# Windowed attention and a gated recurrence on one core: the softmax division moved into the layout of the values product

## What is computed

```python
qkv = einsum('bse,fe->bsf', x, w_in)                   # q, k, v
scores = einsum('bhnqd,bhnkd->bhnqk', q, k2) / sqrt(D) + slope[h] * delta, -inf outside the window
o = einsum('bhnqk,bhnkd->bhnqd', softmax(scores), v2)  # k2, v2: own block and the one before
x1 = layernorm(x + o @ w_out.T)
def step(c, xt):                                        # 16 steps of 512 rows
    ft = sigmoid(xt @ wf.T + c @ uf.T + bf); it = sigmoid(...); gt = tanh(...)
    return ft * c + it * gt
h = tanh(x1 @ wo.T + c_final @ uo.T + bo)
out = layernorm(x1 + h)
```

## Time and profile before

| | before |
|---|---|
| median of 3 runs | 994.17 us (993.75 to 994.33) |
| the profiled execution, its own time | 994.83 us |
| its span | 992.7 us |
| mean granted clock of TensorE | 0.955 |
| TensorE busy | 911.2 us, 92% |
| VectorE busy | 714.1 us, 72% |
| ScalarE busy | 574.8 us, 58% |
| GpSimd busy | 409.0 us, 41% |
| bytes moved | 131.86 MB, mean 133 GB/s |

### The profile page before, as it was taken

How to read it: one execution, slowest core, us unless ns; L and a number is a source line. 1 busy time by engine, 2 the same in 40 slices (tenths; PEclk the granted TensorE clock), 3 DMA queues, 4 the chain that set the end, 5 groups by cost and what they waited for, 6 DMA issues and landing times. The chain is left out here.

```text
span 992.7 us, 25986 instructions
## 1 busy us (share of the span) xinstructions
PE 911.2 (92%) x9500; PEld 749.7 (76%) x9500; DVE 714.1 (72%) x2795; ACT 574.8 (58%) x1167; POOL 409.0 (41%) x687
## 2 busy tenths in 40 slices
PE   3587889999999999999999999999999999989994
PEld 2365668888888888888888888888787876668884
DVE  7666677878787868787878787878787754337875
ACT  6044556565656565656565656565656554335786
POOL 6143343444535353535353535354444443001443
PEclk8586989999999999999999999999999989899998
DMA  7644454535454545353645454645444400131764
GB/s 265 164 124 127 131 139 132 151 122 156 124 151 128 145 134 150 123 154 125 153 128 151 128 143 137 149 131 147 133 121 138 119 23 22 44 106 46 215 204 131
DMA packets 93534, 131.86 MB, mean 133 GB/s; under 512 B 12128, under 2 KB 47584, under 8 KB 93408
## 3 DMA queue, kind: packets, MB, share of 16 engines
q1 hardware_dynamic: 93136, 129.95, 45.3%
q10 hardware_dynamic: 272, 0.26, 0.1%
HBM read 79.31 MB, written 50.33 MB: 131 GB/s over the span
## 5 line engine op out<-in xcount | busy, mean ns | idle before, releaser
L689 DVE CUSTOM_DVE_ANT_0 bank<-bank,mask 128x256 f32<-128x256 f32 (+1 forms) x1024 | 369.4, 423 | 130.7 <-PE bank L951 128.7
L448 ACT ACTIVATE Pt<-bank 128x512 f32<-128x512 f32 (+1 forms) x512 | 248.2, 536 | 193.4 <-PE bank L972 193.3
L347 POOL TENSOR_SCALAR_AFFINE_SELECT Pt<-Pt 128x512 f32<-128x512 f32 x256 | 170.4, 666 | 403.9 <-ACT Pt L448 403.9
L951 PE MATMUL bank<-Ks,Qs 59*128 59x256 f32 (+1 forms) x1024 | 148.2, 319 | 44.9 <-DVE max_q L689 31.3
L951 PEld LDWEIGHTS bank<-Ks,Qs 59*128 59x128 f32 x1024 | 107.3, 191 | 86.6 <-DVE max_q L689 42.5
L689 DVE DVE_READ_ACCUMULATOR2_ANT max_q<- 128x1 f32 x1024 | 144.9, 142 | 0.0
L349 POOL TENSOR_SCALAR_AFFINE_SELECT Pt<-Pt 128x384 f32<-128x384 f32 x256 | 144.7, 565 | 0.0
L986 PE MATMUL bank<-Pt,Vp 128*32 128x256 f32 (+1 forms) x2048 | 130.9, 377 | 0.0
L932 PE MATMUL bank<-x1T,Wg 64*128 64x512 f32 x960 | 127.9, 398 | 1.0 <-DVE o_tok L703 1.0
L932 PE MATMUL bank<-cT,Ug 64*128 64x512 f32 x960 | 125.7, 393 | 0.0
L972 PE MATMUL bank<-Qs,Ks 60*128 60x256 f32 (+1 forms) x1024 | 111.8, 271 | 0.7 <-ACT Pt L448 0.3
(11 more groups left out here) (111 smaller groups left out, 1354.7 us busy)
## 6 DMA issues: line engine op xcount, KB each, us to landing
parts_dram<-qk_parts SPq DMA_DIRECT2D x128, 256.0 KB
Qs<-parts_dram SPq DMA_DIRECT2D x128, 128.0 KB, 2.7
Ks<-parts_dram SPq DMA_DIRECT2D x128, 128.0 KB, 2.8
xt_raw<-in_xt SPq DMA_DIRECT2D x16, 512.0 KB, 4.5
Qs<-parts_dram SPq DMA_DIRECT2D x128, 64.0 KB, 2.7
Ks<-parts_dram SPq DMA_DIRECT2D x128, 64.0 KB, 2.7
x_res<-in_x SPq DMA_DIRECT2D x16, 512.0 KB, 3.9
x_dram<-y SPq DMA_DIRECT2D x16, 512.0 KB, 4.4
```

Source lines behind the costliest of these rows:

```text
L347: gp.affine_select(out=p4[:, :, 0:128], in_=p4[:, :, 0:128], compare_op=ALU.is_ge, fill=0.0, base=0, pattern=[[0, 4], [1, 128]], channel_m ...
L448: sc.activation(probabilities(g, 2 * pair + odd)[:, S * a:S * a + n], SC[odd][:, 0:n], ACT.Exp).then_inc(exp_done, 1)
L689: ins = ve.tensor_tensor_reduce(out=raw, in0=raw, in1=mask[:, keys], scale=1.0, scalar=MASKED, op0=ALU.add, op1=ALU.max, accum_out=max_q[: ...
L951: ins = te.matmul(MX[odd][:, 256 * (n % 2):256 * (n % 2) + 256][:, keys], Qs[rows, 2 * g + pair, n * WIN:(n + 1) * WIN], Ks[rows, 2 * g + ...
```

## The change

1. **Division in the layout of the values product.** `ctx_out` is followed by a store of ctx_raw to DRAM, issued by ScalarE, which waits for its own copy. SP fetches the context rows of two quads at a time into o_un (`load_contexts`) and the denominators, 16 rows for each quarter of a sequence, into den_q (`load_denominators`). VectorE transposes den_q in blocks of 32 x 32, takes reciprocals, transposes back. SP stores the inverses and reads them back, each row spread over the 16 rows of its head (`store_inverses`, `spread_inverses`). GpSimd multiplies (`scale_contexts`), and the product is already in the layout of oT. The context and output transposes of TensorE and `normalise` remain for the last sequence alone.
2. **SP's order.** The inverses go in front of `parts_to_dram(t + 1, 1)`; the second stack goes in front of the next input's load.
3. **Swap.** The second query/key pair is projected in slots 9 and 10, the values projection in slots 11 and 12; the low parts `qk_lo` of the pair stand between the maxima of slots 10, 11 and 12 (before: 12, 13 and 14). The transposes of x1 precede values and maxima in slot 13. Banks are handed on in another rotation.
4. **Input parts.** From sequence 2 on the high parts of x are made two sequences ahead in slots 13 and 14, and the low parts by GpSimd, in front of the last two windows of quad 1.
5. **Buffers and weights.** To make room, Wo and Uo share Win's memory and are loaded and split at the end of the loop, on ScalarE and GpSimd.

```diff
@@ sync
+            def load_denominators(t):
+                sp.wait_ge(den_cleared, 1)
+                for g in range(QUADS):
+                    wait(sp, ctx_stored[g], 16, t, 16)
+                wait(sp, inv_stored, 16, t - 1, 16)
+                rows = ctx_dram[t % 2].rearrange("g (h r) (q i) -> q (g h) r i", r=2 * D, i=128)[:, :, D, :]
+                for q in range(4):
+                    sp.dma_start(den_q[32 * q:32 * q + H, :], rows[q]).then_inc(den_in, 16)
+            def load_contexts(t, c):
+                for g in (2 * c, 2 * c + 1):
+                    wait(sp, ctx_stored[g], 16, t, 16)
+                wait(sp, otlo_done, 2, t - 1, c + 1)
+                rows = ctx_dram[t % 2, 2 * c:2 * c + 2].rearrange("g (h r) s -> (g h) r s", r=2 * D)[:, 0:D, :]
+                sp.dma_start(o_un[:, c, :], rows).then_inc(o_un_in[c], 16)
+            def store_inverses(t):
+                wait(sp, inv_turned, 1, t, 1)
+                sp.dma_start(inv_dram[t % 2].rearrange("r (q i) -> q r i", i=128), den_q[:, :]).then_inc(inv_stored, 16)
+            def spread_inverses(t):
+                wait(sp, inv_stored, 16, t, 16)
+                for c in range(KC):
+                    wait(sp, scaled_done, 2, t - 1, c + 1)
+                    rows = inv_dram[t % 2, 8 * c:8 * c + 8]
+                    sp.dma_start(inv_den[:, c, :], rows.unsqueeze(1).to_broadcast([8, D, S])).then_inc(inv_in[c], 16)
...
+                if now: stack(t, 2)
+                if by_rows: load_contexts(t - 1, 0)
                 if real(t + 2): load_xt(t + 2)
...
+                if by_rows: load_denominators(t - 1)
                 if n1: stack(t + 1, 0)
+                if by_rows: load_contexts(t - 1, 1)
                 if now: max_to_stack(t, 2)
+                if by_rows:
+                    store_inverses(t - 1)
+                    spread_inverses(t - 1)
                 if n1: parts_to_dram(t + 1, 1)
@@ gpsimd
+            def scale_contexts(t, c):
+                wait(pool, o_un_in[c], 16, t, 16)
+                wait(pool, inv_in[c], 16, t, 16)
+                gp.tensor_tensor(o_un[:, c, :], o_un[:, c, :], inv_den[:, c, :], ALU.mult).then_inc(scaled_done, 1)
...
+                    if real(t + 2):
+                        for c in range(KC):
+                            x_lo(t + 2, c)
+                    for hh in range(2, 4):
                         window(t, 1, hh)
@@ scalar
                 sc.activation(ctx_raw[:, :], bank[:, :], ACT.Copy).then_inc(ctx_done, 1)
+                if t < B - 1:
+                    wait(act, ctx_done, 4, t, g + 1)
+                    sc.dma_start(ctx_dram[t % 2, g], ctx_raw[:, :]).then_inc(ctx_stored[g], 16)
...
                 attend(10)
+                if n1: qk_hi(t + 1, 2, A0)
                 attend(11)
-                v_out(t, 0, A0)
+                if n1: qk_hi(t + 1, 3, A1)
                 attend(12)
-                v_out(t, 1, A1)
-                if n1: qk_hi(t + 1, 2, B0)
-                max_row(t, 2, A0)
+                v_out(t, 0, B0)
+                v_out(t, 1, B1)
+                if p2: x1_hi(t - 2, 0, A0)
+                max_row(t, 2, B0)
                 attend(13)
-                if n1: qk_hi(t + 1, 3, B1)
-                ctx_out(t, 0, A1)
-                if p2:
-                    x1_hi(t - 2, 0, B0)
-                    x1_hi(t - 2, 1, B1)
+                if p2: x1_hi(t - 2, 1, A1)
+                ctx_out(t, 0, B1)
+                if real(t + 2): x_hi(t + 2, 0)
                 attend(14)
+                if real(t + 2): x_hi(t + 2, 1)
...
                 exps(t, 3, 3)
+                last_weights_hi()
                 c_hi(t - 2, 0)
@@ vector
                 attend(10)
+                if n1: qk_lo(t + 1, 2, A0)
                 attend(11)
+                if n1: qk_lo(t + 1, 3, A1)
                 attend(12)
-                if n1: qk_lo(t + 1, 2, B0)
                 attend(13)
-                if n1: qk_lo(t + 1, 3, B1)
-                if p1: normalise(t - 1, 3, A0)
+                if p1:
+                    turn_denominators(t - 1)
+                    invert_denominators(t - 1)
+                if p2: x1_lo(t - 2, 0, A0)
+                if p1: turn_inverses(t - 1)
+                if p2: x1_lo(t - 2, 1, A1)
                 attend(14)
```

More of the change, by code:

```diff
@@ L299, in _ @@
             sp.wait_ge(xt_ready, 2 * B)
+            sp.wait_ge(last_lo, 2)
             def load(t, i):
@@ L384, in iteration @@
                         window(t, 0, hh)
-                    for hh in range(4):
+                    for hh in range(2):
+                        window(t, 1, hh)
+                    if real(t + 2):
+                        for c in range(KC):
+                            x_lo(t + 2, c)
+                    for hh in range(2, 4):
                         window(t, 1, hh)
```

306 lines of the change are left out of this document (170 added, 136 removed).

## The result

The changed kernel takes **1022.03 us** (median of 4 runs, 1019.89 to 1032.81) beside 994.25 us for the kernel before on the same chip: ratio 1.0296, 95% interval 1.0221 to 1.037. It is slower by some 28 us, where 974 was forecast. The profiled execution took 1019.89 us.

What follows compares the result with a forecast made beforehand. TensorE's program order was taken to set the 49.9 us period. Per sequence -2.93 + 1.25 + 0.2 = -1.48 us; with start and tail -20.6, from 994.83 to 974.2: forecast 974 us, range 953 to 996.

Steps and rivals of the forecast that it cites:

- Transposes: Context and output transposes leave TensorE's order in slots 0, 5, 8 and 13, saving 2.93 us a sequence.
- the swap: VectorE's low part between the maxima of slots 10 and 11 delays TensorE at slot 12, costing 1.25 us a sequence.
- the trip: SP stores the inverses, waits for landing and spreads them; 3.2 us left for landing, 2.9 taken, so no delay.
- SP's charge: For SP's nine more DMAs and two waits: 0.2 us a sequence, between 0 and 1.
- VectorE: Two transposes and a reciprocal come in slot 13; a transpose taken at 0.3 us, nothing charged, 11 us idle.
- ScalarE's stores: Four context stores a sequence at 0.48 us each, upper end 1.7; cost nothing, little spare before slot 15's scores.
- GpSimd: Two scalings and two input low parts, 5.0 us a sequence, before quad 1's last windows; cost nothing, no cover.
- SP, the step that failed: In SP's queue, inverses land in time and maxima rows aren't delayed; quad 1's stacks keep 0.1 us margin.
- S14 + 8.3: When the next maxima rows are ready, 8.3 us after slot 14's raw scores start; SP's earlier work must be issued.
- the rival with its 5.5 us: Inverses' store landing in 6 us blocks SP, slot 4 waits: 1001 us; slower from 5.5. Chance 0.16, shared.
- ScalarE's issues: ScalarE's store issues at 1.7 us each would end near 1001 us too; chance 0.16 together with the slow landing.
- Ends: Sequence 0 +1.2 us, sequence 1 -0.5, sequence 15 -2.9; tail +0.8, from +1.8 for weight copies and -1.0 for transposes.

Runs made afterwards that it cites:

- run 14: Changed kernel without the inverses' store and spread (constant instead), and with GpSimd's low parts of x behind its last windows: 972.53 us.
- run 8: Changed kernel keeping the inverses' store and SP's wait but without the two spreading DMAs, GpSimd multiplying by a constant: 983.95 us.
- run 1: Changed kernel without the inverses' store and spread, GpSimd multiplying by a constant instead: 981.16 us.
- run 16: Changed kernel; GpSimd issues the spread after its windows, then x's low parts; pair's low parts one slot later; spread rows in turn, context loads reordered: 970.85 us.
- run 12: Changed kernel with the spreads' eight rows read in turn, sixteen times round, not each sixteen times in succession: 1006.95 us.

## Why the prediction was wrong

**Transposes, -2.93 us a sequence, and the swap, +1.25:** right. Period without the trip 48.35, forecast 48.2 without SP's charge; the swap measured 1.21 at its place and slot 0's transposes 1.43 (1.46).

**VectorE:** right. Its transposes, bounded by zero and 0.69 us, taken at 0.3, are these:

```profile
631.99 0.31 DVE L800 STREAM_TRANSPOSE den_t<-den_q 128x128 f32<-128x128 f32 x1
...
633.35 0.30 DVE L809 STREAM_TRANSPOSE den_q<-den_t 128x128 f32<-128x128 f32 x1
```

**ScalarE's stores:** taken at 0.48 us, nearly all took 0.33, and the exponentials weren't late. Right in sign, too dear in size.

**GpSimd:** "Cost nothing, no cover" was right in the steady part and wrong at the start, where the two low parts of x stood 3.6 us waiting for ScalarE's copies with two windows behind them (run 14). The prediction had named the sign of it, a values product that waits for a window.

**SP, the step that failed.** The prediction let the maxima rows be issued on time at S14 + 8.3 and gave the trip 3.2 us. Against its own terms, in the profile: store sent and landed by S14 + 4.8, where 4.05 was allowed (+0.75); spread's issue 1.38 us to the next, not 0.9 (+0.5); part stores 4.34, not 3.33 (+1.0); maxima rows 4.13, not 1.36 (+2.8). Together 5.0 us, which is the delay seen. The first was watched, as the rival with its 5.5 us, and run 8 shows that it alone costs 3 to 5 us in all. The other three are one omission: **a DMA was charged with its own issue, and not with what its bytes do to the issues behind it**, the spreads' 512 KB least of all. The sum also left only 0.3 us between the 1 MB of part stores and the maxima rows, and charged these 1.36 us, the figure of rows that came 6.4 us later. The kernel before has the other case, in the lines of its first part stores above: 2.62 us. So up to 1.6 of the 2.8 us (2.95, the longest of that kind, less 1.36) needs no spread, only rows without a gap; but it was the trip that took the gap away. How the spreads' 512 KB lengthen the issues behind them (part stores, and rows beyond 2.95 us) is seen, and not explained further. The charge of "+0.2, between 0 and 1" was closed upward at 1 by the same omission; the trip measured 3.2 us a sequence (51.59 against 48.35 in run 1).

**The rival that ended on the slower side** (1001, 0.16 with ScalarE's issues) had the right queue and slot 4. It didn't name slot 3, whose wait is the larger (26.3 us against 16.7), and it had the wrong agent: a landing of 6 us, where the store let SyncE go 2.7 to 4.35 us after its issue began. The range ended at 996 and didn't hold the time.

**Ends.** From the fourteenth layernorm to the end the profiles are 3.3 us shorter, where 2.1 was forecast (-2.9 for sequence 15, +0.8 for the tail). The longer wait for ScalarE's layernorm in the tail came: 5.55 us in place of 3.99, forecast +1.8.

```profile
871.91 1.94 PE L1161 MATMUL bank<-ident,y 128*128 128x128 f32 x8 [5.55 <-ACT y L572]
```

The start was forecast at +1.2 for sequence 0 and -0.5 for sequence 1, and is +6.3 in the changed kernel, +4.5 without the trip, +1.6 with the windows first.

Shown: that the spreads cost some 38 us, and that their bytes, their form and their place in the queue share it. The change's own gain, had the trip cost nothing, is that of run 1, 981 us: 7 short of the forecast. In its profile, 3.1 us above the 974.2 that was forecast for a profiled execution, the late start is all of that; the other 4 us are the profile's distance from the median. The 970.85 of run 16 is near the forecast of 974 for another reason, since it holds two edits that the change had not, worth 9 us each by the medians where they were taken on the kernel without the trip. Not shown: how much of run 16 belongs to the loads of the contexts, where 5.7 of the 8.6 us of run 14 lie, and whether the spread's second 19 us are its few DMA engines or the order of its reads.

## What to carry to other kernels

Charge a DMA twice: its issue, and the time for which its bytes keep later issues of the same queue waiting, above all a small urgent one behind it. Where two transfers both have deadlines, look for the queue of an engine with slack before swapping them in one queue. And write a broadcast so that the outermost count of its pattern is 16: the same bytes then cost 15 us less here, though the order of the reads changed with it. When a small DMA moves up in a queue, look in the trace for one that already stands right behind such bytes, and take its price from there.

## What the runs showed of the hardware

- A small DMA issued right behind large ones takes longer to issue. Two of 4 KB took 1.36 us when they came 6.4 us after 1 MB of part stores, 1.9 to 2.95 right behind such stores (both before the change), and 2.4 to 4.1 behind the spreads and the stores. Without the spreads (run 8) they took 1.37 to 1.75 where at least 1.4 us lay between, and 2.3 to 3.3 otherwise.
- 256 KB land in 2.9 us as an ordinary load, in 3.7 as a spread of eight rows in turn by SyncE's queue, in 6.9 by GpSimd's beside the part stores, and in 8.8 there with each row sixteen times in succession.
- The inverses' store has four blocks outermost and (101116 - 99136) / 15 = 132 packets, from runs 8 and 1: 128 and 4. It let its waiter go 2.66 to 4.35 us after its issue began, in thirteen sequences of the change; loads of the same 64 KB land in 2.9. By the rule of the Trainium skill named at run 12 it ran on 4 of the 16 DMA engines, and the 4 further packets agree. A store with 16 outermost wasn't tried.
- GpSimd's issue of the two spreads took 1.31 us of its own time, hardly more than SyncE's 1.27; what it cost was the wait for their landing.
